# Gated attention of a two-layer transformer: the state update and the chunk outputs as three single-pass products of high and low parts

## The chip, the cores and the metric

One core of one Trainium2 chip runs the whole program in one launch. The metric is the device time of that core in microseconds (us).

## The reference

The input is (2, 1024, 512) float32. Four sublayers follow one another, each with a residual and a layer norm: a linear attention, a feed-forward network with 4-bit weights (I = 1408), a gated linear attention, and a feed-forward network over the top half of the tokens by a router's score. The edit lies in the third:

```
q = softmax(x @ Wq.T); k = sigmoid(x @ Wk.T); v = x; gf = log_sigmoid(-k)     # 32 features
for each chunk of 64 tokens, with Bc = cumsum(gf) in the chunk and the state S (32 x 512):
    A[i, j] = sum_d q[i, d] * k[j, d] * exp(Bc[i, d] - Bc[j, d]), kept where j <= i
    o = A @ v + (q * exp(Bc)) @ S
    S = S * exp(Bc[-1]) + (k * exp(Bc[-1] - Bc)).T @ v
go = o @ Wog.T + x @ Wig.T
x = layernorm(x + ((o * rsqrt(mean(o * o) + 1e-5) * w) * (go * sigmoid(go))) @ Wo.T)
```

## The kernel before

Everything is kept as float32. Nearly every large product is made of three single-pass products: an operand is copied by ScalarE to a "high" part of type fp32r, VectorE (or GpSimd) subtracts the high part from the operand and so makes the "low" part, and the tensor engine (TensorE, PE) adds high x high, low x high and high x low in PSUM (`three_products`, lines 41 to 43). A few products take their float32 operands as they are; the trace shows each of these as two instructions.

The second function, `feed_forward_to_end`, holds the feed-forward stretch of block b = 0 to 3 (512 tokens each, 11 gate tiles j), and then the gated attention in blocks n = 0 to 3 of four tiles t of 128 tokens; n = 0, 1 are the first sequence, n = 2, 3 the second. Each engine has its instructions written out in order, and semaphores join them; nothing is reordered, so an instruction that waits holds all that is behind it on its engine.

One tile (n, t), with i = 4n + t, on each engine:

- PE: `transpose_features` (three transposes, L2362 to L2364), in blocks 1 and 2 `transpose_x`, `update` (the state's new part, k_end x x, L2371, which waits until the state before it is ready), `scores` (L2378, which waits for ScalarE's pair_t), then work of others: `project_out` of the block before, or in block 0 `gate_x`; `transpose_o` of the tile before (L2397, which waits for o_lo of an earlier tile); `outputs` (gat x x, L2385, which waits for the mask, and then the query parts x state parts, L2389).
- ScalarE: `take_pairs`, `take_queries`, in blocks 1 and 2 `x_high`, in block 3 twice `upper_half` (a half of the last sublayer's weights), `state_high` (waits for the state), `square_o` and `o_high` of the tile before, `take_o`. In block 0 there come between them: at t = 0 four squares of the feed-forward rows, and at t = 1 `weight_high(WOG)`. In block 3 at t = 1 `pair_weights` follows, with a table load.
- VectorE: `q_low`, `next_state`, `mask`, `x_low` in blocks 1 and 2, `state_low` (waits for `state_high`), then row work: in block 0 normalisation and residuals of the feed-forward rows and `weight_low(WOG)` (t = 2); in block 1 a normalisation; in blocks 1 to 3 the `residual` of block n-1 with its statistics; `o_low` of the tile before; in block 3 `rank`, the router's counts.
- GpSimd: `join_o` behind each `o_low`, `p_low` at the block's end, and the scatter of ranks in block 3.

After the four tiles come the projections of q and k for the next block, the gates `gate_x` and `gate_o` (four 128-wide parts each), and between them the next block's softmax, decays and `features`: key pairs, query pairs, q_state and k_end, whose semaphore s_ft the next block's first transposes await. `gated`, `p_high` and `p_low` make the operand of `project_out`.

For block 0 the features are made in the feed-forward stretch of b = 3 (`FRONT_SUMS + 1`, j = 5).

Of the kernel before, what the change touches and what calls it, by code (L numbers as in the profile page):

```python
# [17 lines left out]
P = 128  # L18
# [917 lines left out]
def feed_forward_to_end(nc, carried, dn_packed, dn_parts, wqkT, wogT, wigT, woT, norm_w, router_w, router_b, x3, score,  # L936
# [15 lines left out]
    with ctx:  # L952
# [30 lines left out]
        w_raw = [put("gw_qk_raw", [P, KC, P], 192)] + [put("gw_raw", [P, KC, C], 64)] * 2 + [put("gwo_raw", [P, KC, C], 124)]  # L983
# [8 lines left out]
        k_end = put("k_end", [P, TB, REP, DK], 74)  # L992
        pair_t = [put(f"pair_t{i}", [2 * DK, 2, P], 84 + i) for i in range(2)]
        q_parts = [put(f"q_parts{i}", [P, P], 102 + i / 2, F32R) for i in range(2)]
        at = [put(f"gat{i}", [P, P], 103 + i / 2) for i in range(2)]
        state = [put(f"state{i}", [P, C], 104 + 2 * i) for i in range(2)]
# [14 lines left out]
        junk_own = put("junk_own", [P, P], 64)  # L1011
# [92 lines left out]
        s_at = sem("scores_masked")  # L1104
        s_su = sem("state_update_done")
# [151 lines left out]
        def _(sp):  # L1257
# [22 lines left out]
            sp.wait_ge(s_gu, KC * (unit(LAST, 3, 0) + 1))  # L1280
            sp.dma_start(w_raw[WIG][:, :, :], wigT).then_inc(s_w[WIG], 16)
            sp.wait_ge(s_wl, 2)
            sp.dma_start(w_raw[WOG][:, :, :], wogT).then_inc(s_w[WOG], 16)
            sp.wait_ge(s_dn, IT * NBLK)
# [52 lines left out]
        def _(act):  # L1337
# [82 lines left out]

            def state_high(n, t):
# [84 lines left out]
            for b in range(NBLK):  # L1506
                for j in range(IT):
# [26 lines left out]
                    if b == LAST and j == FRONT_TOK:  # L1534
                        exponentials(0)
                    if b == LAST and j == SQUARES_LAST:
# [12 lines left out]
            for n in range(NBLK):  # L1549
                for t in range(TB):  # L1550
# [3 lines left out]
                    if 0 < n < LAST:  # L1554
                        x_high(NBLK + n + 1, t)
                    elif n == LAST and t in (1, 2):
                        upper_half(t - 1)
                    state_high(n, t)
# [29 lines left out]
                silu(n, 2)  # L1588
                if n == 2:
# [38 lines left out]
        def _(dve):  # L1628
# [107 lines left out]
            def key_copies(n):  # L1736
                dve.tensor_tensor(k_end[:, :, :, :], copies(ks[:, :, :]), copies(decay[:, 3, :, :]), ALU.mult).then_inc(s_ft, 1)

            def features(n):
                key_pairs(n)  # L1740
                query_pairs(n)
                query_copies(n)
                key_copies(n)
# [10 lines left out]
            def mask(n, t):  # L1754
# [6 lines left out]
                dve.tensor_tensor(at[t % 2][:, :], ps[:, A, 0:P], const.upto[:, :], ALU.mult).then_inc(s_at, 1)  # L1761

# [96 lines left out]
            def rank(b, t):  # L1859
                k = (3 * NT8 - 1) * b + max(0, 3 * t - 1)  # L1860
                s_t = routed[:, NT8 * b + t:NT8 * b + t + 1]
                if t == 0:
                    dve.wait_ge(s_sb, b + 1)
                    dve.wait_ge(s_czero, 1)
# [11 lines left out]
                dve.scalar_tensor_tensor(out=junk_own[:, :], in0=scores[b][:, t * P:(t + 1) * P], scalar=s_t, in1=const.before[:, :],  # L1876
# [69 lines left out]
            for b in range(NBLK):  # L1946
                for j in range(IT):
# [12 lines left out]
                    elif b == LAST and j == FRONT_SUMS + 1:  # L1960
                        query_copies(0)
# [23 lines left out]
                    elif b == LAST and j == FRONT_SUMS + 1:  # L1985
                        key_copies(0)
                        rows.mean_square(dve, b - 1)
            for c in range(KC):
                x_low(NBLK + 1, c)
# [700 lines left out]
```

## Time and profile before

| | |
|---|---|
| median of 3 runs | 941.06 us (940.38 to 942.35) |
| the profiled execution | 941.47 us |
| its span, first to last instruction | 939.5 us |
| mean granted clock of the tensor engine | 0.992 |
| busy share: PE, VectorE, ScalarE, GpSimd | 97%, 69%, 42%, 32% |

The span is what the rows divide; 1.97 us lie around it. A busy share is a mean over the whole span: what an edit is worth is read from the stretch in which it lies, here 534 to 715 us. Matmuls are pipelined, so their durations overlap; the distance of two starts is what one costs.

### The profile page before, as it was taken

What the parts mean: (1) busy time and instruction counts of PE and PEld (TensorE: products, weight loads), DVE (VectorE), ACT (ScalarE), POOL (GpSimd) and SP (SyncE); (2) the same over time, 40 slices, a digit from 0 to 9 for tenths busy, and PEclk for the clock granted to TensorE, in tenths of its full rate; (3) what the DMA queues carried; (4) which work ended last, traced back from release to release, by engine and by line L of the source; (5) the groups of instructions that cost most, each with busy time, mean ns of one, the idle gap of its engine ahead of it and who ended that gap; (6) DMA issues with size and microseconds to landing.
All of it is one profiled execution on the core that took longest, in us unless ns stands there. A gap on an engine that the chain in (4) does not pass through costs nothing.

```text
span 939.5 us, 13836 instructions
## 1 busy us (share of the span) xinstructions
PE 910.0 (97%) x4976; PEld 721.3 (77%) x4976; DVE 647.1 (69%) x1252; ACT 398.7 (42%) x679; POOL 297.9 (32%) x270
## 2 busy tenths in 40 slices
PE   9999999998999999999999989999999999999994
PEld 7778877885787788788767757786867878878883
DVE  6756853578977798798579777757689786464423
ACT  6433122222444634643564566464554364322221
POOL 1000100001876434344234323131226332724343
PEclk9999999999999999999999999999999999999998
DMA  8533101202210000000010110010200543231411
GB/s 282 180 98 118 46 23 46 79 14 83 52 35 1 1 0 1 1 1 1 1 45 1 43 59 1 1 45 1 90 1 24 157 168 112 65 116 58 144 68 45
DMA packets 43973, 54.20 MB, mean 58 GB/s; under 512 B 6113, under 2 KB 25858, under 8 KB 43906
## 3 DMA queue, kind: packets, MB, share of 16 engines
q1 hardware_dynamic: 42082, 49.11, 16.2%
q0 software_dynamic: 1824, 4.22, 1.4%
q8 instruction: 40, 0.66, 0.3%
q14 instruction: 27, 0.22, 0.1%
HBM read 42.78 MB, written 10.52 MB: 57 GB/s over the span
## 4 chain that ended last, share of the span: by engine, by line
PE 64%; DVE 6%; issue 2%; ACT 2%; POOL 1%; DVEq 0%; ACTq 0%; POOLq 0%
PE ps L41 15%; PE ps L43 14%; PE ps L42 14%; PE ps L2283 7%; PE ps L2284 7%; DVE acc L1674 3%; PE ps L2315 1%; PE ps L2385 1%; PE ps L2371 1%; PE ps L2397 1%; ACT acc L1360 1%; PE ps L2378 1%; POOL mh_lo L2247 0%; PE ps L2346 0%; PE ps L2521 0%
## 5 line engine op out<-in xcount | busy, mean ns | idle before, releaser
L1674 DVE SCALAR_TENSOR_TENSOR acc<-ps,gu_scale,acc 128x512 f32<-128x512 f32 x264 | 197.0, 748 | 52.9 <-ACT acc L1360 33.8
L2283 PE MATMUL ps<-xt_hi,gu_val 128*128 128x512 f32 x352 | 141.5, 402 | 6.0 <-PEq L71 2.5
L2284 PE MATMUL ps<-xt_lo,gu_val 128*128 128x512 f32 x352 | 137.2, 390 | 0.0
L1360 ACT ACTIVATE acc<-ps,gu_scale 128x512 f32<-128x512 f32 x88 | 60.6, 689 | 97.2 <-PE ps L2284 97.1
L2187 POOL TENSOR_TENSOR fsg<-fsg,acc 128x512 f32<-128x512 f32 x44 | 59.0, 1341 | 113.3 <-DVE acc L1674 109.3
L2283 PEld LDWEIGHTS ps<-xt_hi,gu_val 128*128 128x128 f32 x352 | 66.0, 187 | 34.5 <-DVE acc L1674 19.2
L661 POOL TENSOR_TENSOR a_rstd<-a_var,minus_half 128x1 f32<-128x1 f32 x15 | 9.8, 652 | 210.1 <-DVE a_var L544 210.1
L2284 PEld LDWEIGHTS ps<-xt_lo,gu_val 128*128 128x128 f32 x352 | 66.1, 188 | 11.9
L2192 POOL TENSOR_TENSOR fh_lo<-fsg,fh_hi 128x512 fp32r<-128x512 f32 x44 | 57.5, 1306 | 42.9 <-ACT fh_hi L1372 42.9
L41 PE MATMUL ps<-dn_hi,fh_hi 128*128 128x512 f32 x176 | 69.3, 394 | 0.0
L43 PE MATMUL ps<-dn_lo,fh_hi 128*128 128x512 f32 x176 | 68.6, 390 | 0.0
L42 PE MATMUL ps<-dn_hi,fh_lo 128*128 128x512 f32 x176 | 68.6, 390 | 0.0
L2247 POOL TENSOR_TENSOR mh_lo<-mh,mh_hi 128x512 fp32r<-128x512 f32 x32 | 41.6, 1302 | 76.8 <-ACT mh_hi L1613 76.5
L1608 ACT ACTIVATE mh<-ps,b_sb 128x512 f32<-128x512 f32 x32 | 22.0, 687 | 96.7 <-PE ps L43 93.9
L41 PE MATMUL ps<-a_w_hi,xt_hi 128*128 128x512 f32 x128 | 51.9, 405 | 0.0
L41 PE MATMUL ps<-mxt_hi,mw_hi 128*128 128x512 f32 x128 | 50.3, 393 | 1.0 <-DVE mxt_lo L1886 1.0
L41 PE MATMUL ps<-mw_hi,mh_hi 128*128 128x512 f32 x128 | 50.0, 390 | 0.2 <-POOL mh_lo L2247 0.2
L43 PE MATMUL ps<-a_w_lo,xt_hi 128*128 128x512 f32 x128 | 49.9, 390 | 0.0
L42 PE MATMUL ps<-a_w_hi,xt_lo 128*128 128x512 f32 x128 | 49.9, 390 | 0.0
L43 PE MATMUL ps<-mw_lo,mh_hi 128*128 128x512 f32 x128 | 49.8, 389 | 0.0
L43 PE MATMUL ps<-mxt_lo,mw_hi 128*128 128x512 f32 x128 | 49.8, 389 | 0.0
L42 PE MATMUL ps<-mw_hi,mh_lo 128*128 128x512 f32 x128 | 49.8, 389 | 0.0
(292 smaller groups left out, 2164.9 us busy)
## 6 DMA issues: line engine op xcount, KB each, us to landing
mw_raw<-in_w SPq DMA_DIRECT2D x16, 512.0 KB, 3.6
a_nib<-in_gate_up_packed SPq DMA_DIRECT2D x88, 64.0 KB, 2.4
x<-x SPq DMA_DIRECT2D x16, 256.0 KB, 2.8
mw_raw<-x SPq DMA_DIRECT2D x8, 512.0 KB, 4.4
out<-mw_raw SPq DMA_DIRECT2D x8, 512.0 KB, 2.9
xt_raw<-in_xT SPq DMA_DIRECT2D x3, 1024.0 KB, 5.1
x<-in_x SPq DMA_DIRECT2D x3, 1024.0 KB, 5.8
a_nib<-in_down_packed SPq DMA_DIRECT2D x8, 256.0 KB, 3.0
```

Source lines behind the costliest of these rows:

```text
L41: pe.matmul(out, lh, rh, start=first, stop=False)
L42: pe.matmul(out, ll, rh, start=False, stop=False)
L43: return pe.matmul(out, lh, rl, start=False, stop=last)
L661: pool.tensor_tensor(rstd[i % 2][:, :], var[i % 2][:, :], const.minus_half[:, 0:1], ALU.pow).then_inc(s_rstd, 1)
L1360: act.activation(acc[part][u // 2 % 2][:, :], ps[:, FG, :], ACT.Copy, scale=gu_scale[:, part * IT + j, 0:1]).then_inc(s_g0, 1)
L1608: act.activation(h[j % 2][:, :], ps[:, H + j % 4, :], ACT.Gelu_apprx_tanh, bias=b1_sb[:, j:j + 1]).then_inc(m_g, 1)
L1674: dve.scalar_tensor_tensor(out=a[:, :], in0=ps[:, FG + c, :], scalar=gu_scale[:, part * IT + j, c:c + 1], in1=a[:, :], op0=ALU.mult, op1=A ...
L2187: pool.tensor_tensor(f_sg[k % 2][:, :], f_sg[k % 2][:, :], acc[1][k % 2][:, :], ALU.mult).then_inc(s_h, 1)
L2192: pool.tensor_tensor(f_lo[k % HS][:, :], f_sg[k % 2][:, :], f_hi[k % HS][:, :].bitcast(F32), ALU.subtract).then_inc(s_hl, 1)
L2247: pool.tensor_tensor(h_lo[j % HS][:, :], h[j % 2][:, :], h_hi[j % HS][:, :].bitcast(F32), ALU.subtract).then_inc(m_hl, 1)
L2283: pe.matmul(ps[:, FG + c, :], gu_val[:, o, c, :], xt_hi[b % 2][:, c, :], start=True, stop=False)
L2284: pe.matmul(ps[:, FG + c, :], gu_val[:, o, c, :], xt_lo[b % 2][:, c, :], start=False, stop=True).then_inc(s_gu, 1)
```

## The change

The product k_end x x of `update` and the product gat x x of `outputs` become three single-pass products each. For this k_end is split into k_hi and k_lo, the masked scores into at_hi and at_lo, and the rows of x into x_part_hi and x_part_lo, two buffers each for tiles in turn.

- ScalarE: `x_part_high` of the next tile and `scores_high` of this one stand ahead of `state_high`; `key_high` of the next block behind `silu(n, 2)`.
- VectorE: `x_part_low` of the next tile and `scores_low` stand behind `mask`; `key_copies` (128x512) becomes `key_ends` (128x128), and `key_low` (128x512) comes ahead of `gated(n, 2)`.
- PE: `update` also waits for x_part_lo, `outputs` for at_lo in place of the mask.
- For room, the raw weights of the two gates lie where their low parts will be. The input gate's load is issued one group of products later, and the output gate's behind the last down projection instead of behind the input gate's low part. junk_own has a buffer for each batch, and `rank` waits for the last features.

```diff
@@ -980,7 +980,7 @@
         w_at = [(188, 190), (94, 86), (76, 108), (116, 124)]
-        w_raw = [put("gw_qk_raw", [P, KC, P], 192)] + [put("gw_raw", [P, KC, C], 64)] * 2 + [put("gwo_raw", [P, KC, C], 124)]
+        w_raw = [put("gw_qk_raw", [P, KC, P], 192)] + [put(f"gw_raw{i}", [P, KC, C], w_at[i][1]) for i in (WIG, WOG, WO)]
         w_hi = [put(f"gw_hi{i}", [P, KC, w_cols[i]], w_at[i][0], F32R) for i in range(NW)]
@@ -989,10 +989,15 @@
         q_state = put("q_state", [P, TB, REP, DK], 72)
-        k_end = put("k_end", [P, TB, REP, DK], 74)
+        k_hi = put("k_hi", [P, TB, REP, DK], 74, F32R)
+        k_lo = put("k_lo", [P, TB, REP, DK], 194, F32R)
+        x_part_hi = [put(f"x_part_hi{i}", [P, C], 64 + 2 * i, F32R) for i in range(2)]
+        x_part_lo = [put(f"x_part_lo{i}", [P, C], 68 + 2 * i, F32R) for i in range(2)]
         pair_t = [put(f"pair_t{i}", [2 * DK, 2, P], 84 + i) for i in range(2)]
...
         at = [put(f"gat{i}", [P, P], 103 + i / 2) for i in range(2)]
+        at_hi = [put(f"gat_hi{i}", [P, P], 196 + i / 2, F32R) for i in range(2)]
+        at_lo = [put(f"gat_lo{i}", [P, P], 103 + i / 2, F32R) for i in range(2)]
         state = [put(f"state{i}", [P, C], 104 + 2 * i) for i in range(2)]
@@ -1008,7 +1013,7 @@
         rw_sb = put("rw_sb", [P, C], 192)
-        junk_own = put("junk_own", [P, P], 64)
+        junk_own = [put(f"junk_own{b}", [P, P], at_) for b, at_ in enumerate((197, 64))]
@@ -1102,6 +1107,12 @@
         s_at = sem("scores_masked")
+        s_ath = sem("scores_hi_done")
+        s_atl = sem("scores_lo_done")
+        s_kf = sem("k_end_ready")
+        s_kh = sem("k_end_hi_done")
+        s_xph = sem("x_part_hi_done")
+        s_xpl = sem("x_part_lo_done")
         s_su = sem("state_update_done")
@@ -1277,11 +1288,10 @@
                 down_scale(j)
-            sp.wait_ge(s_gu, KC * (unit(LAST, 3, 0) + 1))
+            sp.wait_ge(s_gu, KC * (unit(LAST, 3, 1) + 1))
             sp.dma_start(w_raw[WIG][:, :, :], wigT).then_inc(s_w[WIG], 16)
-            sp.wait_ge(s_wl, 2)
+            sp.wait_ge(s_dn, IT * NBLK)
             sp.dma_start(w_raw[WOG][:, :, :], wogT).then_inc(s_w[WOG], 16)
-            sp.wait_ge(s_dn, IT * NBLK)
             sp.dma_start(w_raw[WO][:, :, :], woT).then_inc(s_w[WO], 16)
@@ -1418,6 +1428,25 @@
+            def x_part_high(n, t):
+                i = TB * n + t
+                if i >= 2:
+                    act.wait_ge(s_o, i - 1)
+                act.wait_ge(rows.s_out, TB * n + t + 1)
+                act.activation(x_part_hi[t % 2][:, :], x[n][:, t, :], ACT.Copy).then_inc(s_xph, 1)
+
+            def scores_high(n, t):
+                i = TB * n + t
+                act.wait_ge(s_at, i + 1)
+                if i >= 2:
+                    act.wait_ge(s_o, i - 1)
+                act.activation(at_hi[t % 2][:, :], at[t % 2][:, :], ACT.Copy).then_inc(s_ath, 1)
+
+            def key_high(n):
+                act.wait_ge(s_kf, n + 1)
+                act.wait_ge(s_su, TB * n)
+                act.activation(k_hi[:, :, :, :], qx[:, :, :].unsqueeze(2).to_broadcast([P, TB, REP, DK]), ACT.Copy).then_inc(s_kh, 1)
+
             def state_high(n, t):
@@ -1533,6 +1562,10 @@
                         exponentials(0)
+                    if b == LAST and j == FRONT_SUMS + 1:
+                        key_high(0)
+                    if b == LAST and j == IT - 1:
+                        x_part_high(0, 0)
                     if b == LAST and j == SQUARES_LAST:
@@ -1555,6 +1588,9 @@
                         upper_half(t - 1)
+                    if n < LAST or t + 1 < TB:
+                        x_part_high(n + (t + 1) // TB, (t + 1) % TB)
+                    scores_high(n, t)
                     state_high(n, t)
@@ -1586,6 +1622,8 @@
                 silu(n, 2)
+                if n < LAST:
+                    key_high(n + 1)
                 if n == 2:
@@ -1733,14 +1771,19 @@
-            def key_copies(n):
-                dve.tensor_tensor(k_end[:, :, :, :], copies(ks[:, :, :]), copies(decay[:, 3, :, :]), ALU.mult).then_inc(s_ft, 1)
+            def key_ends(n):
+                dve.wait_ge(s_qn, 3 * n + 3)
+                dve.tensor_tensor(qx[:, :, :], ks[:, :, :], decay[:, 3, :, :], ALU.mult).then_inc(s_kf, 1)
+
+            def key_low(n):
+                dve.wait_ge(s_kh, n + 1)
+                dve.tensor_tensor(k_lo[:, :, :, :], copies(qx[:, :, :]), k_hi[:, :, :, :].bitcast(F32), ALU.subtract).then_inc(s_ft, 1)
...
                 query_pairs(n)
+                key_ends(n)
                 query_copies(n)
-                key_copies(n)
@@ -1759,6 +1802,16 @@
                 dve.tensor_tensor(at[t % 2][:, :], ps[:, A, 0:P], const.upto[:, :], ALU.mult).then_inc(s_at, 1)
+
+            def scores_low(n, t):
+                i = TB * n + t
+                dve.wait_ge(s_ath, i + 1)
+                dve.tensor_tensor(at_lo[t % 2][:, :], at[t % 2][:, :], at_hi[t % 2][:, :].bitcast(F32), ALU.subtract).then_inc(s_atl, 1)
+
+            def x_part_low(n, t):
+                i = TB * n + t
+                dve.wait_ge(s_xph, i + 1)
+                dve.tensor_tensor(x_part_lo[t % 2][:, :], x[n][:, t, :], x_part_hi[t % 2][:, :].bitcast(F32), ALU.subtract).then_inc(s_xpl, 1)
@@ -1861,6 +1914,7 @@
                     dve.wait_ge(s_sb, b + 1)
+                    dve.wait_ge(s_ft, NBLK)
                     dve.wait_ge(s_czero, 1)
@@ -1873,7 +1927,7 @@
                     dve.wait_ge(s_cnt, k - 2)
-                dve.scalar_tensor_tensor(out=junk_own[:, :], in0=scores[b][:, t * P:(t + 1) * P], scalar=s_t, in1=const.before[:, :],
+                dve.scalar_tensor_tensor(out=junk_own[b][:, :], in0=scores[b][:, t * P:(t + 1) * P], scalar=s_t, in1=const.before[:, :],
                                          op0=ALU.is_equal, op1=ALU.mult, accum_out=counts[:, 2, t:t + 1]).then_inc(s_cnt, 1)
@@ -1958,6 +2012,7 @@
                     elif b == LAST and j == FRONT_SUMS + 1:
+                        key_ends(0)
                         query_copies(0)
@@ -1983,16 +2038,20 @@
                     elif b == LAST and j == FRONT_SUMS + 1:
-                        key_copies(0)
+                        key_low(0)
                         rows.mean_square(dve, b - 1)
...
                 x_low(NBLK + 1, c)
+            x_part_low(0, 0)
             weight_low(WIG)
...
                     mask(n, t)
+                    if n < LAST or t + 1 < TB:
+                        x_part_low(n + (t + 1) // TB, (t + 1) % TB)
+                    scores_low(n, t)
                     if 0 < n < LAST:
@@ -2046,6 +2105,8 @@
                     folded_low(range(2, KC))
+                if n < LAST:
+                    key_low(n + 1)
                 gated(n, 2)
@@ -2368,7 +2429,9 @@
                     pe.wait_ge(s_sb, 1)
-                pe.matmul(ps[:, S, :], k_end[:, t, :, :].rearrange("p r d -> p (r d)"), x[n][:, t, :], start=True, stop=True).then_inc(s_su, 1)
+                pe.wait_ge(s_xpl, i + 1)
+                k_parts = [k[:, t, :, :].rearrange("p r d -> p (r d)") for k in (k_hi, k_lo)]
+                three_products(pe, ps[:, S, :], *k_parts, x_part_hi[t % 2][:, :], x_part_lo[t % 2][:, :], True, True).then_inc(s_su, 1)
@@ -2380,9 +2443,10 @@
                 first = n % 2 == 0 and t == 0
-                pe.wait_ge(s_at, i + 1)
+                pe.wait_ge(s_atl, i + 1)
                 pe.wait_ge(s_ot, i)
-                ins = pe.matmul(ps[:, O, :], at[t % 2][:, :], x[n][:, t, :], start=True, stop=first)
+                ins = three_products(pe, ps[:, O, :], at_hi[t % 2][:, :], at_lo[t % 2][:, :], x_part_hi[t % 2][:, :], x_part_lo[t % 2][:, :],
+                                     True, first)
                 if not first:
...
                     pe.wait_ge(s_sl, i)
```

## Rows read from the trace of the kernel before

**Rows 1.** The page: busy time, share of the span and instructions of each engine.
```profile
PE 910.0 (97%) x4976; PEld 721.3 (77%) x4976; DVE 647.1 (69%) x1252; ACT 398.7 (42%) x679; POOL 297.9 (32%) x270
```

**Rows 2.** Waits from 530 to 720 us: who waited for whom: total us, times, longest.
```profile
DVE s_parts L1779 <- ACT s_parts L1426: 3.9, 8, 0.5
...
PE ps L2378 <- ACT pair_t L1410: 2.0, 3, 1.3
...
PE ps L2397 <- DVE o_lo L1785: 1.2, 1, 1.2
...
DVE gw_lo L1679 <- ACT gw_hi L1340: 0.8, 1, 0.8
```

**Rows 3.** PE in order of time, block 0: start, us, instruction.
```profile
538.91 0.39 PE L43 MATMUL ps<-xt_lo,gw_hi 128*128 128x512 f32 x1
539.13 1.02 PE L2385 MATMUL ps<-x,gat 128*128 128x512 f32 x2
539.99 0.27 PE L2362 MATMUL ps<-ident,k_pair 128*64 128x128 f32 x1
```

**Rows 4.** Groups by line and shape, 534 to 720 us: busy us, mean ns, idle.
```profile
L1761 DVE TENSOR_TENSOR gat<-ps,upto 128x128 f32<-128x128 f32 x16 | 4.5, 284 | 0.1
...
L1737 DVE TENSOR_TENSOR k_end<-ks,decay 128x512 f32<-128x512 f32 x3 | 2.1, 684 | 0.0
...
L1426 ACT ACTIVATE s_parts<-state 128x512 fp32r<-128x512 f32 x16 | 10.1, 632 | 22.2 <-DVE state L1772 19.9 <-DVE state L1769 2.3
...
L1419 ACT ACTIVATE q_parts<-ps 128x128 fp32r<-128x128 f32 x16 | 4.2, 265 | 0.0
```

**Rows 5.** PE in order of time, block 0; in brackets the wait before.
```profile
541.81 0.48 PE L2378 MATMUL ps<-pair_t 64*128 64x128 f32 x2 [0.47 <-ACT pair_t L1410]
...
548.20 0.48 PE L2378 MATMUL ps<-pair_t 64*128 64x128 f32 x2 [0.22 <-ACT pair_t L1410]
...
560.67 0.63 PE L2397 MATMUL ps<-ident,o_tok 128*128 128x128 f32 x4 [1.17 <-DVE o_lo L1785]
...
562.71 0.80 PE L41 MATMUL ps<-o_hi,gw_hi 128*128 128x512 f32 x1 [0.97 <-DVE o_lo L1785]
```

**Rows 6.** VectorE in order of time, block 0, behind the residuals of its last tile.
```profile
559.85 0.67 DVE L1785 TENSOR_TENSOR o_lo<-ps,o_hi 128x512 fp32r<-128x512 f32 x1
```

**Rows 7.** VectorE, GpSimd and PE in order of time, end of block 0.
```profile
571.04 1.73 POOL L2115 TENSOR_TENSOR p_lo<-gsg,p_hi 128x512 fp32r<-128x512 f32 x1 [6.06 <-ACT p_hi L1473]
...
571.54 1.78 DVE L1797 TENSOR_TENSOR gsg<-gsg,o_f 128x512 f32<-128x512 f32 x1
...
582.95 1.29 POOL L2115 TENSOR_TENSOR p_lo<-gsg,p_hi 128x512 fp32r<-128x512 f32 x1 [1.29 <-ACT p_hi L1473]
...
584.29 0.50 PE L41 MATMUL ps<-gw_hi,p_hi 128*128 128x512 f32 x1
```

**Rows 8.** Busy time of each engine in a tile of blocks 1, 2, 3, and behind.
```profile
594.01:600.54 6.53, 6.53 (x32) 4.50 (x30) 5.39 (x12) 3.35 (x9) 1.27 (x2) 1.00 0.00 0
640.15:646.60 6.45, 6.45 (x31) 4.49 (x30) 4.84 (x10) 3.26 (x9) 0.35 (x1) 1.00 0.00 1
...
702.73:709.48 6.75, 6.75 (x31) 4.58 (x30) 6.07 (x17) 3.00 (x8) 4.64 (x5) 1.00 0.02 5
...
715.00:760.00 45.00, 45.00 (x210) 37.48 (x209) 38.21 (x87) 19.57 (x28) 21.92 (x18) 1.00 0.39 123
```

**Rows 9.** PE and VectorE in order of time, block 3, tiles 1 to 3.
```profile
697.27 0.28 DVE L1761 TENSOR_TENSOR gat<-ps,upto 128x128 f32<-128x128 f32 x1
...
698.09 1.02 PE L2385 MATMUL ps<-x,gat 128*128 128x512 f32 x2
...
701.82 0.49 PE L2378 MATMUL ps<-pair_t 64*128 64x128 f32 x2 [1.29 <-ACT pair_t L1410]
...
711.62 1.02 PE L2385 MATMUL ps<-x,gat 128*128 128x512 f32 x2
```

**Rows 10.** As rows 8, one microsecond of block 0's end (third figure from the right: granted clock).
```profile
563.00:564.00 1.00, 1.00 (x3) 0.81 (x3) 0.26 (x1) 0.99 (x2) 1.00 (x2) 0.50 0.00 0
```

## The prediction

> **What bounds the kernel now.** I read the page first, then the tensor engine's waits in the gated-attention stretch (530 to 720 us), then the order of time of each engine there. The page shows the tensor engine busy for 97% of the span and the vector engine for 69% [rows 1]. Taken alone, that says: a shorter product shortens the kernel. But it is a mean. The edit lies in one stretch, four blocks of four tiles, and there the tensor engine's few waits are all behind ScalarE or VectorE: 2.0 us for pair_t, 1.2 us for o_lo [rows 2], 0.97 us more for o_lo at 562.71 [rows 5]. So the question is, block by block, which queue ends last once the tensor engine's list is shorter and the other two are longer.
>
> **The products.** Matmuls overlap, so I take starts, not durations. The float32 product of gat (L2385, two instructions) starts at 539.13 and the next instruction at 539.99: 0.86 us. A single-pass product of the same shape starts 0.22 to 0.23 us behind the one before it (538.91 to 539.13) [rows 3]. Three of them are 0.68 us, so a product gains 0.86 - 0.68 = 0.18, say 0.175 us. There are 16 tiles with two such products: 32 x 0.175 = 5.6 us is the most the tensor engine can give. The lower bound is nothing (the three parts might start as the first product behind a float32 one does, a third of a microsecond apart).
>
> **The new work.** For each tile but the first, the part of x: ScalarE copies 128x512 (nearest row s_parts, 632 ns), VectorE subtracts 128x512 (nearest k_end, 684 ns). For each tile, the masked scores: ScalarE 128x128 (q_parts, 265 ns), VectorE 128x128 (nearest gat, 284 ns) [rows 4]. From start to start VectorE takes some 0.08 us less where it does not wait, so a tile costs it 0.6 + 0.2 to 0.69 + 0.28, that is 0.8 to 0.97 us; I take 0.9. All of it stands in an in-order queue between the mask and x_low or state_low. The ends of keys: once a block, the 128x512 product becomes a 128x128 one (+0.28), a ScalarE copy (+0.63) and a 128x512 subtraction (the same 0.68): 0.28 us more for VectorE, under the tensor engine's last gate products, 24 x 0.23 = 5.5 us, whose cover is ample. x_part of tile 0 and the halves of key 0 fall in the feed-forward stretch or in the 0.8 us in which VectorE waits for gw_hi [rows 2]: nothing. Of the weight loads, the input gate's is issued one group of products later, seven gate tiles ahead of its user, and the other two no longer wait behind its lower half: nothing. Their lower halves now overwrite the raw ones, same shapes: nothing. The extra wait on s_ft before a rank stands behind its own producer: nothing.
>
> **Block 0: +1.2 us.** Here the tensor engine already waits, so its gain is lost and the added work shows. At t = 0 ScalarE now waits for the mask (0.28) and copies it (0.27, less an overlap) ahead of state_high and the four squares, behind which take_o and pair_t stand: pair_t at 541.81 comes 0.5 us later. At t = 1 the subtraction of x and the chain mask, scores_high, state_high delay it again: 548.20 becomes 549.04, +0.84 [rows 5]. At t = 3 VectorE sets the end: q_low starts 0.85 late, since the delayed tile 2 and a full weight_low stand in front of it; the two subtractions add 0.85, and 0.5 is won back, since state_low waits for s_parts 0.5 us in most tiles [rows 2] and would find it done. o_low at 559.85 [rows 6] comes at 561.05, and the tensor engine's waits at 560.67 and 562.71 [rows 5] move by 1.2. Bounds: +0.5 (only the scalar shift stays) and +1.6.
>
> **Block 1: -0.6 us.** The first tile starts badly: p_lo ends at 582.95 + 1.29 = 584.24 and the tensor engine takes it at 584.29 [rows 7], so nothing is gained in front of it, and gated(2) is 0.2 late behind key_low. In the tiles VectorE is busy 5.39 of 6.53 us [rows 8]. With the additions it needs 5.39 + 0.9 = 6.3 us, where the tensor engine would need 6.53 - 0.35 = 6.18. VectorE becomes the bound by a little: 4 x (6.53 - 6.33) = 0.8, less 0.2 at the start. Bounds: -1.4 and 0.
>
> **Block 2: -1.4 us.** No normalisation lies in these tiles: 4.84 + 0.9 = 5.7 us of VectorE [rows 8] under 6.1. The whole 8 x 0.175 is kept. Bounds: -1.4 and -0.9.
>
> **Block 3: +0.8 us.** The ranks of the router stand in the tiles; VectorE is busy 6.07 of 6.75 us [rows 8], while the tensor engine's own tile is shorter than block 1's, since no x is transposed. In tile 1 the mask starts at 697.27 and outputs at 698.09 [rows 9]. Afterwards the mask is 0.35 late (0.85 added in tile 0, the 0.5 of s_parts [rows 2] won back), so at 697.6; it takes 0.2, the subtractions 0.6 and 0.25: outputs start at 698.7, +0.6. Their end is 0.4 late, and take_o, the table load, pair_t behind it: 701.82 becomes 702.2. By tile 3 VectorE has lost three times some 0.3 to 0.35, and the mask, the scores' copy and their subtraction follow: outputs at 711.62 [rows 9] move by 1.0, of which the product gives 0.18 back. Bounds: 0 and +1.6. Behind this the tensor engine is busy 45.0 of 45.0 us [rows 8], so the shift stays.
>
> **The sum** is 1.2 - 0.6 - 1.4 + 0.8 = 0.0. The profiled execution took 941.47 us for a span of 939.5; the median of the runs is 941.06. I predict 941.0.
>
> **A port that two engines share.** An operation of VectorE of this shape takes 0.68 us [rows 4], but the product gsg of two SBUF tiles takes 1.78 us at 571.54, while GpSimd's p_lo runs from 571.04 to 572.77 [rows 7]. The new subtractions are such operations too. The nearest GpSimd work in a tile is join_o, 1.27 us from the end of o_low; the new ones start q_low + state + mask = 1.5 us behind it, so by rows they miss it. The Trainium skill, page VectorE: DVE Perf Modes, section Two Vector instructions with no wait between them, names the second SBUF read interface, through which the second of two SBUF inputs is read, as shared with GpSimd; it gives no delay, and the trace shows one, 1.78 against 0.68. By that rule without regard to place the sum would be that of the rival "shared port" below.
>
> **The rivals.**
> *The full gain.* The vector queue gives way: the waits of block 0 and 3 are absorbed, and the products' gain arrives. For it: 97% of the tensor engine, 69% of the vector engine [rows 1]. Against: the waits that stand there already [rows 2]. With all of it -5.6 us, 935.5; with half 938.3. Chance 0.24.
> *The clock falls once more.* After the waits at 560.67 and 562.71 the granted clock is 0.50 [rows 10], the lower level of 1.2 GHz, for about 3.3 us up to 566, where products start 0.43 apart instead of 0.23. That costs 1.6 us and is in the time of before. The edit makes new gaps: 1.5 us near 541, 1.1 near 548, 1.0 near 698 and 1.6 near 701. Against it: a gap of 1.29 us at 701 [rows 9] left the clock at full. It decides if one more such stretch occurs: 0 + 1.6, with a larger shift of block 0 up to +3: 942.6 to 944. This is the case on the other side. Chance 0.20.
> *Shared port.* If the x subtractions meet join_o as gsg met p_lo, 0.7 us each; 11 of the 15 lie in blocks 0, 1 and 3 where VectorE decides: up to +7.7, 948. Against: the 1.5 us distance. Chance 0.06.
> *The products gain nothing.* If three parts cost 0.86 us, block 0 and 3 keep their losses, and blocks 1 and 2 give nothing: 1.2 + 0 + 0 + 1.1 = +2.3, 943.4. Chance 0.05.
> *The forecast*, gains eaten by the vector queue, 941.0, own range 939.4 to 942.6: chance 0.45.
>
> **Range and chances.** Faster or slower by 0.2% is 1.9 us, about what a measurement of this kernel tells from none. Faster: the full gain and a little of the forecast's edge, 0.26. Slower: the clock, the port and the lost gain, less their small cases, 0.28. The rest, 0.46, is no difference. The range reaches half of the full gain and past it, 937.5, and the larger clock case, 944.3.
>
> **What the changed profile would show.** L2371 and L2385 gone; three single-pass products each, 0.23 us apart. A wait of PE on at_lo's VectorE line in blocks 0 and 3, of about 1 us at 698 and 712; the wait for o_lo of 560.67 grown from 1.2 towards 2 us; VectorE without idle time in the tiles of block 1; no PE wait in block 2. I am wrong if the tiles of block 3 are no longer than before (then the queue had room), or if a second stretch at 0.50 stands in the clock's row.

## The result, and the profile after

The changed kernel takes 942.74 us (median of 20 runs, 941.5 to 944.33) against 941.03 us of the kernel before (20 runs, 939.63 to 942.96). The ratio is 1.0017, interval 1.0011 to 1.0024: 1.7 us slower. That is inside the prediction's range, and smaller than the 0.2% that it counts as no difference. But the interval lies clear of 1: the kernel did become slower, where the forecast was a sum of 0.0, and that sum is what has to be explained.

The page of the changed kernel, busy time of each engine, for comparison with [rows 1]:

```profile
PE 904.9 (96%) x5008; PEld 726.1 (77%) x5008; DVE 659.5 (70%) x1288; ACT 412.1 (44%) x715; POOL 299.1 (32%) x270
```

The tensor engine's busy time fell by 5.1 us, VectorE's and ScalarE's rose by 12.4 and 13.4. The kernel did not become shorter, so what the tensor engine gained went into waits. Not all of the 5.1 us is the edit: in the profile of before two short stretches ran at the lower clock, where the same work is busy for longer (mean granted clock 0.57 from 64 to 68 us, 0.50 in [rows 10]), and the changed kernel's has neither. This view shows who waited for whom from 530 to 725 us (total us, times, longest):

```profile
PE ps L2441 <- ACT pair_t L1420: 4.3, 5, 1.4
PE ps L41 <- DVE gat_lo L1809: 1.9, 4, 0.9
PE ps L2461 <- DVE o_lo L1838: 1.7, 1, 1.7
...
PE ps L41 <- DVE o_lo L1838: 1.0, 1, 1.0
PE ps L2423 <- DVE k_lo L1780: 0.8, 1, 0.8
...
PE ps L41 <- POOL p_lo L2176: 0.4, 1, 0.4
```

The waits of [rows 2], 2.0 for pair_t (ScalarE's copy of the transposed features) and 1.2 for o_lo (the low part of a tile's output), have grown to 4.3 and 1.7, and new ones stand beside them: for gat_lo (the masked scores' low part), for k_lo (the keys' low part) and for p_lo.

To see where each block gains or loses, I take the same instruction of every block in both traces: the first transposes of the features, k_pair, of each block, and the transposes of the routed rows, xsel, behind it all. The marks lie at 534.46, 579.79, 633.04, 687.45 and 740.46 us before and at 535.98, 582.31, 635.61, 688.90 and 743.20 after. The last column is what the forecast had.

| block | before, us | after, us | change | forecast |
|---|---|---|---|---|
| 0 | 45.33 | 46.33 | +1.00 | +1.2 |
| 1 | 53.25 | 53.30 | +0.05 | -0.6: +0.2 up to its p_lo, -0.8 behind it |
| 2 | 54.41 | 53.29 | -1.12 | -1.4 |
| 3 | 53.01 | 54.30 | +1.29 | +0.8 |
| stretch | 206.00 | 207.22 | +1.22 | 0.0 |

The profiled execution of after took 944.33 us, the longest of its 20. 1.52 us of its longer span lie ahead of the stretch: its mark is at 535.98 against 534.46. In all fourteen profiles (these two and one of each experiment below) that mark lies between 532.98 and 536.20, in no order that follows the edits, so I compare stretches and not spans.

Blocks 0 and 1 of the changed kernel, the tensor engine in order of time, against [rows 5] and the last line of [rows 7]; the mark of before comes first:

```profile
534.46 0.27 PE L2362 MATMUL ps<-ident,k_pair 128*64 128x128 f32 x1 [1.00 <-ACT y_sb L863]
...
535.98 0.27 PE L2423 MATMUL ps<-ident,k_pair 128*64 128x128 f32 x1 [0.99 <-ACT y_sb L863]
...
543.85 0.48 PE L2441 MATMUL ps<-pair_t 64*128 64x128 f32 x2 [1.32 <-ACT pair_t L1420]
...
550.64 0.48 PE L2441 MATMUL ps<-pair_t 64*128 64x128 f32 x2 [0.95 <-ACT pair_t L1420]
...
563.69 0.63 PE L2461 MATMUL ps<-ident,o_tok 128*128 128x128 f32 x4 [1.73 <-DVE o_lo L1838]
...
565.73 0.50 PE L41 MATMUL ps<-o_hi,gw_hi 128*128 128x512 f32 x1 [0.98 <-DVE o_lo L1838]
...
582.31 0.30 PE L2423 MATMUL ps<-ident,k_pair 128*64 128x128 f32 x1 [0.83 <-DVE k_lo L1780]
...
584.32 0.49 PE L2441 MATMUL ps<-pair_t 64*128 64x128 f32 x2 [0.36 <-ACT pair_t L1420]
...
587.49 0.50 PE L41 MATMUL ps<-gw_hi,p_hi 128*128 128x512 f32 x1 [0.41 <-POOL p_lo L2176]
588.71 0.50 PE L41 MATMUL ps<-x_part_hi,gat_hi 128*128 128x512 f32 x1 [0.24 <-DVE gat_lo L1809]
```

Counted from the mark (subtract 535.98 here, 534.46 before), pair_t is 0.52 and then 0.92 later than before, o_lo 1.50, and the product that takes block 1's last p_lo 51.51 - 49.83 = 1.68. The transpose at 582.31 waits 0.83 us for k_lo. VectorE around it:

```profile
579.43 0.29 DVE L1776 TENSOR_TENSOR qx<-ks,decay 128x128 f32<-128x128 f32 x1
...
580.25 1.41 DVE L1722 SCALAR_TENSOR_TENSOR gw_lo<-gw_raw,norm_w_sb,gw_hi 128x512 fp32r<-128x512 f32 x2
581.57 0.68 DVE L1780 TENSOR_TENSOR k_lo<-qx,k_hi 128x512 fp32r<-128x512 f32 x1
582.17 0.68 DVE L1850 TENSOR_TENSOR gsg<-gsg,o_f 128x512 f32<-128x512 f32 x1
```

The keys' source was there at 579.7; k_lo stands behind 1.41 us of folded weights (gw_lo), and gsg, the operand of the next block's projection, stands behind k_lo.

Busy time of each engine, as in [rows 8]: first the place where before lost its clock [rows 10], then a tile of block 1 and one of block 3 (from q_low to q_low, 697.84 to 704.99):

```profile
562.00:566.00 4.00, 1.34 (x9) 1.13 (x10) 2.49 (x7) 2.26 (x6) 1.53 (x2) 1.00 0.00 0
...
597.48:603.70 6.22, 6.22 (x33) 4.86 (x32) 6.03 (x14) 4.07 (x11) 1.29 (x1) 1.00 0.00 0
697.84:704.99 7.15, 5.17 (x26) 3.71 (x25) 6.87 (x18) 5.39 (x12) 1.62 (x2) 1.00 0.00 0
```

Block 1's tile is 6.22 us instead of 6.53, and VectorE is busy in 6.03 of it: the two queues are almost equal. Block 3's tile is 7.15 us instead of 6.75, with VectorE busy in 6.87 of it. The granted clock is 1.00 at 562 to 566, the upper level of 2.4 GHz, although the waits in front of it are longer than before.

Inside a block 1 tile, the new products:

```profile
601.13 0.48 PE L41 MATMUL ps<-x_part_hi,gat_hi 128*128 128x512 f32 x1
601.45 0.40 PE L42 MATMUL ps<-x_part_hi,gat_lo 128*128 128x512 f32 x1
601.68 0.40 PE L43 MATMUL ps<-x_part_lo,gat_hi 128*128 128x512 f32 x1
601.92 0.39 PE L2453 MATMUL ps<-s_parts,q_parts 128*128 128x512 f32 x1
```

The second and third start 0.23 us apart, as forecast; behind the first it is 0.32. And in block 3 the tensor engine waits for the scores' low part, and for pair_t between:

```profile
700.27 0.50 PE L41 MATMUL ps<-x_part_hi,gat_hi 128*128 128x512 f32 x1 [0.54 <-DVE gat_lo L1809]
...
703.93 0.48 PE L2441 MATMUL ps<-pair_t 64*128 64x128 f32 x2 [1.45 <-ACT pair_t L1420]
...
714.46 0.50 PE L41 MATMUL ps<-x_part_hi,gat_hi 128*128 128x512 f32 x1 [0.89 <-DVE gat_lo L1809]
```

### The profile page after: what moved, and what is told of

It reads as the page before. It is cut to its first block, busy times and chain, and to the rows that moved or that the text cites. A ratio compares the mean times of both kernels' runs of the same rounds, so it can differ in the third digit from the quotient of the medians.

```text
span 942.3 us, 14019 instructions
## 1 busy us (share of the span) xinstructions
PE 904.9 (96%) x5008; PEld 726.1 (77%) x5008; DVE 659.5 (70%) x1288; ACT 412.1 (44%) x715; POOL 299.1 (32%) x270
## 4 chain that ended last, share of the span: by engine, by line
PE 59%; DVE 9%; ACT 3%; issue 3%; POOL 1%; DVEq 0%; ACTq 0%; POOLq 0%
PE ps L41 14%; PE ps L43 14%; PE ps L42 14%; PE ps L2344 7%; PE ps L2345 7%; DVE acc L1712 3%; PE ps L2376 1%; ACT acc L1370 1%; DVE state L1825 1%; PE ps L2461 1%; ACT fjunk L870 0%; DVE gsg L1850 0%; DVE junk L1925 0%; DVE q_parts L1794 0%; POOL mh_lo L2308 0%
```

## The experiments

Two theories stood against each other. **Queue**: the tensor engine's gain is real, and the queues of VectorE and ScalarE take it back, block by block. **Rivals**: the products gain little or nothing; the new places and loads cost; an engine's shared path or the clock costs. The edits below are shown against the changed kernel, that of experiment 10 against the kernel before. Kernels run together share their runs of the kernel before: 940.69 us for the first four, 941.08 for the next four, 940.33 for the last four.

**1. Only the places and loads.** Buffers and DMA order of the changed kernel, the work of the one before. A pair of sets says in which blocks the update (U3) and the outputs (O3) are split; here it is none.

```diff
+        U3, O3 = set(), set()
...
+                if n not in O3:
+                    return
                 act.wait_ge(s_at, i + 1)
```

> Both products in float32 and no halves, as before; kept of the edit are only the new places of the raw gate weights, the later issue of their loads, the junk buffers and the wait of rank. Theory A (the edit lost by the work that it adds to VectorE's and ScalarE's queues): no change, ratio 0.9995 to 1.0005. Theory B (the loads or the places cost, or the clock of the changed program differs for another reason): about the 1.0017 of the edit.

Measured 940.33 us (12 runs), ratio 0.9999 (0.999 to 1.0008). Loads and places cost nothing that can be seen; what moved the time is work.

**2. Only the products.** The mask writes at_hi and the key copies write k_hi at once, the same part stands for high and low, and one fixed tile of x stands for all. So this kernel leaves out the low parts and the true rows of x.

```diff
+                k_parts = [k[:, t, :, :].rearrange("p r d -> p (r d)") for k in (k_hi, k_hi)]
+                three_products(pe, ps[:, S, :], *k_parts, x_part_hi[0][:, :], x_part_hi[0][:, :], True, True).then_inc(s_su, 1)
```

> The products are three single-pass ones, but no half is made: the ends of keys and the masked scores are rounded once and stand in for both of their parts, and one fixed tile of x stands in for all, so this leaves out the low parts and the true rows of x. Theory A: the tensor engine's gain without its price; block 0 is bound by others as before, blocks 1 to 3 keep 24 x 0.175 = 4.2 us, less 0.2 to 1 us at waits that stay: -3.2 to -4.4 us, ratio 0.9953 to 0.9966. Rival (three products cost what one float32 product costs): ratio 1.000.

Measured 938.98 us (11 runs), ratio 0.9982 (0.9972 to 0.9992): 1.7 us instead of the 3.2 to 4.4 expected. The profile says where: block 0 -0.10, blocks 1 and 2 -1.24 and -1.27, block 3 -0.59. That is 3.2 us in the stretch of this one execution, more than the runs have in their median. Their mean granted clock is lower (0.9916 over the 11 runs, 0.9936 over the 28 of before), which may be where the rest went; no run here shows it. Eight products a block gain 1.25, so 0.156 each. In block 0 even the bare products give next to nothing, and in block 3 half of that, since the tensor engine only arrives earlier at its wait for pair_t. Its waits, without any low part being made in the tiles:

```profile
PE ps L2452 <- ACT pair_t L1420: 3.1, 4, 1.6
PE ps L2472 <- DVE o_lo L1849: 1.4, 1, 1.4
...
PE ps L41 <- DVE o_lo L1849: 1.0, 1, 1.0
```

**3. Only the work.** The parts are made, the products stay float32, of the high parts alone (the low parts are left out of the result).

```diff
+                pe.matmul(ps[:, S, :], k_hi[:, t, :, :].rearrange("p r d -> p (r d)").bitcast(F32), x[n][:, t, :], start=True, stop=True).then_inc(s_su, 1)
...
+                ins = pe.matmul(ps[:, O, :], at_hi[t % 2][:, :].bitcast(F32), x[n][:, t, :], start=True, stop=first)
```

> All halves are made and waited for, but the products are float32 ones of the high parts (the low parts are left out of the result). Theory A: the price without the gain; by the after-trace some 1.5 us in block 0, 2 at its end, 0.5 to 1 in block 1, 0 in block 2, 1.5 in block 3: +4 to +6 us, ratio 1.0043 to 1.0064, and together with the run without halves it gives about the measured 1.0017. Theory B: +1.7 us or less.

Measured 945.31 us (6 runs), ratio 1.0043 (1.0029 to 1.0057). That is 4.0 us, the lower end of the 4 to 6 expected. By blocks: +1.01, +1.18, -0.02, +1.49. Set beside the second experiment the two sides add up to the edit within 0.2 us in blocks 0 to 2 and within 0.4 in block 3:

| block | products only | work only | their sum | both (the edit) |
|---|---|---|---|---|
| 0 | -0.10 | +1.01 | +0.91 | +1.00 |
| 1 | -1.24 | +1.18 | -0.06 | +0.05 |
| 2 | -1.27 | -0.02 | -1.29 | -1.12 |
| 3 | -0.59 | +1.49 | +0.90 | +1.29 |

By the measured ratios 0.9982 x 1.0043 = 1.0025, and the edit's is 1.0017. The work costs something in three blocks of four and nothing in block 2, the one whose tiles hold neither a normalisation nor ranks for VectorE.

**4. Only the outputs.** The update stays as before in all blocks, so no keys are split (O3 all four, U3 none).

> Only the outputs are three products; the state update stays float32 with full k_end, so no key halves; x and score halves are made as in the edit. Theory A: the same 0.9 us a tile on VectorE, half the gain (2.8 us at most, 1.4 to 2 kept), but no k_lo in front of gated at the end of block 0 (about -1): +2 to +3 us, ratio 1.002 to 1.0032. Theory B: 1.0015 to 1.002 whatever is left out.

Measured 943.47 us (12 runs), ratio 1.0027 (1.0017 to 1.0036), as expected: half of the products' gain with nearly all of the tile's added work. Whether it is dearer than the edit the runs do not tell; the two intervals overlap. The start of block 1 is what it was run for:

```profile
564.54 0.50 PE L41 MATMUL ps<-o_hi,gw_hi 128*128 128x512 f32 x1 [0.98 <-DVE o_lo L1867]
...
582.94 0.49 PE L2473 MATMUL ps<-pair_t 64*128 64x128 f32 x2 [1.02 <-ACT pair_t L1430]
...
586.11 0.50 PE L41 MATMUL ps<-gw_hi,p_hi 128*128 128x512 f32 x1 [0.42 <-POOL p_lo L2205]
```

Its mark is at 534.80, so o_lo lets the tensor engine go at 29.74 (the edit: 29.75), and the product that takes the last p_lo starts at 51.31 (the edit: 51.51). No key is split here, and there is no wait for k_lo. So the key halves cost 0.20 us at this place, and the 0.83 us wait for k_lo is not added to them: without it the tensor engine waits 1.02 for pair_t instead of 0.36.

**5 and 6. The edit in blocks 1 and 2 alone; in blocks 0 and 3 alone.**

```diff
+        U3, O3 = {1, 2}, {1, 2}
```

> Three products and their halves in blocks 1 and 2 alone; blocks 0 and 3 as before. Theory A (the loss sits in blocks 0 and 3 and at the end of block 0): block 0 nothing but the x part of block 1's first tile and its key halves (+0.6, and up to 0.8 of a wait for k_lo), block 1 about 0, block 2 -1.1: 0.0 to -0.8 us in the stretch. Rival (every tile loses alike): half of the edit's loss, +0.6 to +0.9.

> Three products and their halves in blocks 0 and 3 alone. Theory A: the waits for pair_t and o_lo in block 0 (+1.5, against which the clock may stay high as in the edit's profile, -1.3), block 3 +1.3: +1.3 to +2.8 us, worse than or like the whole edit. Rival: half of the edit's loss, +0.6 to +0.9.

Blocks 1 and 2: 939.54 us (8 runs), ratio 0.9976 (0.9965 to 0.9987), more gained than expected. Blocks 0 and 3: 944.05 us (12 runs), ratio 1.0024 (1.0015 to 1.0033), as expected. The same edit is a gain in one half of the blocks and a loss in the other: the cause sits in what else the queues hold.

**7. gated(0, 2) ahead of the key and weight halves.** All work is done, in another order on VectorE.

```diff
                 if n == 0:
+                    gated(n, 2)
+                    key_low(n + 1)
                     folded_low(range(2, KC))
-                if n < LAST:
-                    key_low(n + 1)
-                gated(n, 2)
+                else:
+                    if n < LAST:
+                        key_low(n + 1)
+                    gated(n, 2)
```

> The edit, with VectorE's order at the end of block 0 changed: gated(0,2) straight behind the features, then key_low, then the low parts of the output weights. Theory A (key_low behind two weight operations delays the tensor engine by 0.8 us and, through gated and silu, pair_t and p_lo by 0.4 each): the waits for k_lo, pair_t, p_lo at block 1's start go: -1.2 to -1.8 us against the edit, +0 to +0.5 against before. Rival (these waits only take the place of one another): no change against the edit, 1.0017.

Measured 941.64 us (11 runs), ratio 1.0004 (0.9995 to 1.0013): by the ratios 1.2 us less than the edit, the lower end of the 1.2 to 1.8 expected. The stretch of its profile is only 0.77 us shorter. The waits at the start of block 1 show why, in order of time:

```profile
580.40 0.30 PE L2426 MATMUL ps<-ident,k_pair 128*64 128x128 f32 x1 [0.17 <-DVE k_lo L1780]
...
582.75 0.50 PE L41 MATMUL ps<-gw_hi,p_hi 128*128 128x512 f32 x1 [0.28 <-DVE gw_lo L1722]
...
585.39 0.50 PE L41 MATMUL ps<-gw_hi,p_hi 128*128 128x512 f32 x1 [0.28 <-POOL p_lo L2179]
586.59 0.50 PE L41 MATMUL ps<-x_part_hi,gat_hi 128*128 128x512 f32 x1 [0.24 <-DVE gat_lo L1809]
```

The 0.83 for k_lo fell to 0.17, and 0.28 for the folded weights came up in its place. Three arrivals lie within a few tenths of each other. The product that takes the last p_lo comes at 585.39 - 534.70 = 50.69 instead of 51.51.

**8. The low part of x on GpSimd**, so that VectorE's tile loses 0.6 us.

```diff
+            def x_part_low(n, t):
+                i = TB * n + t
+                pool.wait_ge(s_xph, i + 1)
+                pool.tensor_tensor(x_part_lo[t % 2][:, :], x[n][:, t, :], x_part_hi[t % 2][:, :].bitcast(F32), ALU.subtract).then_inc(s_xpl, 1)
```

> The edit, with the low part of x made by GpSimd (1.3 us each, idle there) in place of VectorE. Theory A (VectorE's queue sets the loss): the wait for o_lo 0.6 to 0.9 shorter, the waits for gat_lo in block 3 gone: -1.5 to -2.5 us against the edit, so -0.8 to +0.2 against before. Rival (ScalarE's copies and the chain mask, copy, state_high set it): no more than -0.5. Rival (the shared port): VectorE's two-input operations stretch under GpSimd and the run is slower than the edit.

Measured 944.64 us (8 runs), ratio 1.0032 (1.0019 to 1.0045), against 1.0017 of the edit. The intervals overlap a little; in the profiles the stretch is 2.63 us longer than the edit's, so it is slower. VectorE's groups by line and shape, 536 to 716 us, are in this kernel:

```profile
L1827 DVE TENSOR_TENSOR s_parts<-state,s_parts 64x512 fp32r<-64x512 f32 x16 | 11.4, 713 | 1.5 <-ACT s_parts L1455 1.1
...
L1809 DVE TENSOR_TENSOR gat_lo<-gat,gat_hi 128x128 fp32r<-128x128 f32 x16 | 8.1, 505 | 6.1 <-ACT gat_hi L1443 6.1
```

In the edit gat_lo takes 285 ns in the mean, with 0.4 us of idle time in all. Two things happened. VectorE cannot make gat_lo before ScalarE has copied the scores, so it now waits 0.38 us in each of 16 tiles, 6.1 us in all; in the edit the low part of x fills just that gap. And gat_lo is stretched where GpSimd works beside it:

```profile
597.66 0.28 DVE L1804 TENSOR_TENSOR gat<-ps,upto 128x128 f32<-128x128 f32 x1
598.33 0.80 DVE L1809 TENSOR_TENSOR gat_lo<-gat,gat_hi 128x128 fp32r<-128x128 f32 x1 [0.38 <-ACT gat_hi L1443]
```

That one takes 0.80 us while GpSimd's subtraction of x runs from 597.67 to 598.97. Of the 0.6 us a tile moved away, 0.38 comes back as a wait and 0.22 as a stretch in the mean (0.505 - 0.285).

**9. Experiments 5 and 7 together.**

> Three products in blocks 1 and 2 alone, and gated(0,2) ahead of key_low and the low weight parts. Theory A (blocks 0 and 3 have no room on VectorE and ScalarE, and the end of block 0 is a chain through gated): another 0.6 to 1.0 us below the run with blocks 1 and 2 alone, -2.0 to -3.2 us against before, ratio 0.9966 to 0.9979. Rival (the waits only change places): 0.9976 as that run.

Measured 938.26 us (11 runs), ratio 0.998 (0.9971 to 0.9989). Beside 0.9976 of experiment 5 the order adds nothing that can be told from the runs; the stretch of the profile is 0.87 us shorter than experiment 5's.

**10. The kernel before with that order.**

```diff
+                gated(n, 2)
                 if n == 0:
                     folded_low(range(2, KC))
-                gated(n, 2)
```

> The kernel before with gated(0,2) ahead of the low weight parts and nothing else: how much of the gain of that order belongs to the edit. Theory A: the tensor engine waits at block 1's start for 0.2 us of p_lo alone, so 0 to -0.3 us, ratio 0.9997 to 1.0. Rival (the chain through gated sets the start of block 1 in the kernel before too, behind the slow clock): -0.8 us, 0.9991.

Measured 939.88 us (11 runs), ratio 0.9997 (0.9987 to 1.0006). In its profile the clock stayed at 1.00 through 562 to 570, and block 0 took 43.82 us instead of 45.33, the stretch 1.64 us less; over the runs no such gain can be seen.

**11. The edit in block 2 alone.**

> Three products and halves in block 2 alone, where no queue is full. Theory A: eight products gain 0.14 each, -1.1 us in the stretch, ratio 0.9985 to 0.9991. If block 1 gives nothing (its own gain against the waits at its first tile), this equals the run with blocks 1 and 2, in the stretch within 0.3 us.

Measured 939.42 us (11 runs), ratio 0.9987 (0.9978 to 0.9997), as expected. In its profile block 2 has 53.28 us instead of 54.41.

**12. state_high ahead of scores_high on ScalarE.**

```diff
+                    state_high(n, t)
                     scores_high(n, t)
-                    state_high(n, t)
```

> The edit with ScalarE's state_high ahead of scores_high. Theory A (part of block 0's loss is that state_high and the squares wait for the mask and its copy): pair_t of tiles 1 and 2 some 0.3 us earlier, o_lo at the end of block 0 0.3 earlier, gat_lo no later, since x_part_low covers the round trip: -0.3 to -0.6 us against the edit, ratio 1.0011 to 1.0014. Rival (VectorE's queue alone counts): as the edit, 1.0017; and if gat_lo comes later, slower.

Measured 942.53 us (10 runs), ratio 1.0022 (1.0012 to 1.0031): not the gain that was expected. The waits of 530 to 725 us:

```profile
PE ps L2441 <- ACT pair_t L1420: 3.8, 5, 1.4
PE ps L41 <- DVE gat_lo L1809: 2.7, 4, 1.2
PE ps L2461 <- DVE o_lo L1838: 1.8, 1, 1.8
```

pair_t comes earlier, its total falls by 0.5 us; the wait for gat_lo grows by 0.8. In its profile block 3 up to the last transposes of o takes 30.02 us instead of 29.33.

## Why the forecast was wrong, and which terms were mis-sized

**What failed.** The forecast was no difference, the sum 1.2 - 0.6 - 1.4 + 0.8 = 0.0. The runs show a loss of 1.7 us (1.0 to 2.3 by the interval), the stretch of the two profiles 1.22. The step that failed is the size of the terms: the losses of blocks 0 and 3 were put too small and the gains of blocks 1 and 2 too large, and the balance of 0.0 rested on them. In the prediction's own terms, counted from each block's mark:

| term | forecast | measured | miss |
|---|---|---|---|
| block 0, up to its last o_lo | +1.2 | +1.50 | +0.30 |
| from there to block 1's last p_lo (gated behind key_low) | +0.2 | +0.18 | -0.02 |
| block 1 behind that p_lo (48.75 to 48.12) | -0.8 | -0.63 | +0.17 |
| block 2 | -1.4 | -1.12 | +0.28 |
| block 3 | +0.8 | +1.29 | +0.49 |
| sum | 0.0 | +1.22 | +1.22 |

**What held** is the mechanism: the tensor engine's gain is eaten by the vector and scalar queues, lost in blocks 0 and 3, kept in block 2, nearly even in block 1. Experiments 2 and 3 show the two sides separately, and 5 and 6 show them by place. The two shifts of pair_t (0.5 and 0.84 forecast, 0.52 and 0.92 measured) and "the extra loads: nothing" hold. The signs named beforehand are there: the wait for gat_lo at 700 and 714, o_lo's from 1.17 to 1.73, no wait in block 2. VectorE in a block 1 tile, 6.3 us by the forecast, is busy 6.03 and goes from q_low to q_low in 6.29 (598.27 to 604.56), beside 6.22 on the tensor engine.

*"Block 3: +0.8"* is the largest miss. The VectorE tile grew by 0.4 us (starts of q_parts at 697.84, 704.99 and 712.16: 7.15 and 7.17, before 6.75) where 0.3 to 0.35 was taken. The mask of tile 3 comes 1.24 late, counted from block 3's mark, the way from the mask over ScalarE's copy to outputs(3, 3) takes 1.00 instead of 0.85, so the outputs come 1.39 late instead of 1.0; and the product gives back 0.10 instead of 0.18. Before, then after:

```profile
710.77 0.28 DVE L1761 TENSOR_TENSOR gat<-ps,upto 128x128 f32<-128x128 f32 x1
711.55 0.69 DVE L1779 TENSOR_TENSOR s_parts<-state,s_parts 64x512 fp32r<-64x512 f32 x1 [0.50 <-ACT s_parts L1426]
...
699.13 0.28 DVE L1804 TENSOR_TENSOR gat<-ps,upto 128x128 f32<-128x128 f32 x1
699.34 0.68 DVE L1814 TENSOR_TENSOR x_part_lo<-x,x_part_hi 128x512 fp32r<-128x512 f32 x1
699.93 0.28 DVE L1809 TENSOR_TENSOR gat_lo<-gat,gat_hi 128x128 fp32r<-128x128 f32 x1
700.31 0.69 DVE L1832 TENSOR_TENSOR s_parts<-state,s_parts 64x512 fp32r<-64x512 f32 x1
...
713.46 0.28 DVE L1804 TENSOR_TENSOR gat<-ps,upto 128x128 f32<-128x128 f32 x1
```

From the mask to s_parts it is 0.78 before and 1.18 after: +0.40, where the forecast had 0.85 less 0.5. Part of it is a start that the forecast did not price. From x_part_lo to gat_lo a start is 0.59, less than its 0.68; gat_lo takes 0.28, but s_parts starts 0.38 behind it. s_parts covers 64 partitions, the upper half. The Trainium skill, page VectorE: DVE Perf Modes, section Two Vector instructions with no wait between them, says that an instruction whose operands start in another group of 32 partitions than the last ones is held until all earlier ones have finished; the row agrees, with 0.10 us behind the end instead of 0.09 ahead of it.

*"Block 0: +1.2"*. The forecast let q_low of tile 3 start 0.85 late and took 0.35 more for what stands between mask and s_parts; they are 1.09 (19.82 to 20.91 behind the mark) and 0.40. Before, then after:

```profile
554.28 0.59 DVE L1751 TENSOR_TENSOR q_parts<-ps,q_parts 32x128 fp32r<-32x128 f32 x2 [0.26 <-ACT q_parts L1419]
...
556.89 0.59 DVE L1794 TENSOR_TENSOR q_parts<-ps,q_parts 32x128 fp32r<-32x128 f32 x2
```

*"A product gains 0.175"*. It gains 0.155: a tile with two falls from 6.53 [rows 8] to 6.22 us, and experiment 2 gives 1.25 for eight. The sum took 0.225 for each of three starts, but the start after the first product, which stands behind a float32 instruction, is 0.32 (601.13 to 601.45). The prediction had this third of a microsecond in its bound and not in its value. For eight products it is 0.16 of the 0.28 missing in block 2; experiment 3 finds no price of the work there (-0.02), so the rest stays open.

*Block 1.* Its later tiles gain more than the 0.2 each of the forecast (6.53 to 6.22), but the first loses: the tensor engine waits 0.24 us for gat_lo, and the second tile's transposes come 2.25 us behind the product that takes p_lo instead of 1.90.

*"The ends of keys: 0.28 us more for VectorE, whose cover is ample"*. The cover was measured on the wrong queue. The tensor engine's 5.5 us of gate products hide the key halves' length, but the halves stand behind folded_low and ahead of gated(0, 2), on a VectorE queue that is 1.50 late already, and the result is a wait of 0.83 for k_lo at 582.31 that the forecast did not have. Its price was right all the same: 0.18 in the edit, 0.20 by experiment 4.

**Luck.** Block 0's +1.00 stands near the forecast's +1.2 for other reasons: it is the +1.50 of o_lo, less 1.33 by which the tensor engine is faster behind it, at full clock, plus the 0.83 of waiting for k_lo.

**The clock.** *The clock falls once more*: it did not. In the stretch before has one fall to 0.50 [rows 10], 1.2 GHz; after has none, at longer waits (1.73 and 0.98). The prediction says that the fall costs 1.6 us and is in the time of before. The profiles show that it costs nothing there. From the product that waits for the second o_lo to the one that takes block 1's last p_lo:

| kernel | clock behind o_lo | us |
|---|---|---|
| before | falls to 0.50 | 21.58 |
| experiment 1 | falls to 0.50 | 21.57 |
| experiment 4, no key halves | full | 21.57 |
| the edit | full | 21.76 |
| experiment 5 | full | 21.78 |
| experiment 7, the edit with gated(0, 2) first | full | 20.92 |
| experiment 10, before with gated(0, 2) first | full | 19.99 |

With the order of before it takes the same time at either level: the chain through VectorE's gsg, p_hi and p_lo ends last there, and what the tensor engine gains by the full clock it spends in waiting for k_lo, pair_t and p_lo. Whether the clock falls differs between kernels with the same work ahead of 562 us (it falls in before and in experiments 1 and 11, not in 10), so I draw no cause for it.

**The other rivals.** *The full gain* is out: experiment 2, without any of the added work in the tiles, has 1.7 us by its runs and 3.2 by its profile, where the largest forecast gain was 5.6. The other products stand in front of waits. *Shared port*: not in the edit, where x_part_lo takes 681 ns in the mean. Its price is real, as experiment 8 shows once GpSimd's work is put there. *The products gain nothing* is out by experiment 2 and by block 2.

**What beats both kernels** is experiment 5 (or 9): the edit where VectorE has room, 0.9976 and 0.998.

**Open.** Why block 3 of the edit is 0.39 us dearer than products and work added up, and block 2 0.17. Why the runs of experiments 2 and 10 show 1.7 and 0.3 us where the stretches of their profiles show 3.2 and 1.6; one profile stands for one execution, and differences of a few tenths of a microsecond in the block tables rest on one execution of each kernel.

## What to carry to other kernels

Price a split into high and low parts per stretch, by the in-order queue that ends last there, and put it only where that queue has room: the same edit is worth 0.9976 in two blocks and 1.0024 in the other two. When gains and losses nearly cancel in your sum, a few hundredths of a microsecond a tile decide it: take the added time from start to start between the same two instructions, not from the durations. A wait in the profile is not its price either: follow the latest arrival behind it. Here a wait of 0.83 us came and a half-speed stretch of the tensor engine went, and the first cost 0.2 us and the second gave nothing back, since p_lo arrived later than both. And before you move work off a full engine, look for the round trip that it fills: what stands between an operand and its copy by another engine may cost nothing where it is.

## What the runs showed of the hardware

- A single-pass product starts 0.23 us behind another, but 0.32 behind one that itself followed a float32 instruction (601.13 to 601.45; the median of 34 such starts in the changed kernel from 570 to 735 us). Going from the one kind to the other costs about 0.1 us each time.
- A VectorE subtraction of two SBUF operands, 128x128, takes 0.28 us alone and 0.80 beside a GpSimd operation of the same kind, nearly three times as long.
- The mask, ScalarE's copy of it and the return to VectorE leave VectorE idle for 0.38 us if nothing stands between.
- The granted clock stayed full behind waits of 1.73 and 0.98 us (after), and fell behind 1.17 and 0.97 us (before): the length of the two gaps alone did not decide it. At the lower level products start 0.43 us apart instead of 0.23 (before, 564.16 to 564.59).
